# A planner that orders five engine queues: its durations, a price on idle TensorE, and other preferences among streams

## The chip, the cores and the metric

The kernel runs on one core of one Trainium2 chip. The metric is the time of one execution on the device in microseconds, lower is better. Each kernel's time is the median of several runs.

## The reference

One transformer layer on `x` of shape (2, 4096, 256) in float32, with one attention head of width 256, followed by a layer that processes only three quarters of the rows (cut):

```
qkv = x @ w_attn + b_attn; q, k, v = split(qkv, 3)
attn = softmax(q @ k.T / sqrt(256) + causal_mask)
x = layernorm(x + (attn @ v) @ w_proj + b_proj)
scores = x @ w_router
_, top_idx = top_k(scores, k=3072)            # of 4096 rows in each batch
out = x.at[top_idx].set(gelu(x[top_idx] @ w_block))
return layernorm(x + out)
```

## The kernel before

The work is cut into 16 groups: two batches of eight, each of 512 queries. Group g of a batch has 4(g+1) tiles of 128 keys by 512 queries, 288 tiles in all. Every float32 operand of the big products is split into a high and a low part, and three products (low by high, high by high, high by low) stand for one, so a tile of scores is six matmuls of up to 512 columns (L535, into one of two `sbank` banks), and a tile of values is six as well (L1134 to L1136, into `obank`; the first three groups of a batch use L1128 to L1130).

A group goes through these stages. *Project*: ScalarE and GpSimd split the rows of `x` (`xT`), TensorE makes queries and values (L535 into `fbank`). *Scores*: TensorE writes a bank, ScalarE copies it into one of 34 slots of `ring` (L955), VectorE masks it and keeps a running maximum (L992, L997). *Row maximum*: four transposes (L1030), a VectorE reduction, four transposes back (L1053). *Softmax*: VectorE subtracts (L1066), ScalarE takes the exponential (L1073) and rounds it to the high part (`parts`, L1080), VectorE makes the low part (`ring_lo`, L1085). *Values*: SyncE loads 256 KB per tile of keys into one of six slots (`vs`, L1103), TensorE multiplies. *Attention out*: ScalarE empties `obank` (L1194), residual, layer norm, router score. *ffn*: TensorE multiplies by `w_block` (L535 with `WB`), gelu on ScalarE, sum with `x1` on GpSimd (L1556), statistics on VectorE; `x1` and `y` go to scratch memory in DRAM. The 512-KB load of the residual rows of group G (L1177, stream "attention_out load") waits until GpSimd has made the sums of group G - 2 (`g_y`), because they share a buffer.

After the last group of a batch, a *search* finds the 3072nd largest router score in eight rounds: VectorE compares (L1668), TensorE counts with a matrix of ones (L1724), VectorE adds up and decides (L1679, L1685). Then rows are picked (L1917) and stored. The scratch rows of the second batch come back during the last group's values (`final_load`: two loads of 256 KB, L1850 and L1851, inside the stream "values load", one pair for every three tiles).

What the five engines do in which order isn't written by hand. Each step is put into a named *stream* of an engine (`at("act", "softmax exp", exp)`), and the order inside a stream is fixed. Before anything is emitted, `merged` lets every step run against a `Rehearsal` object that adds up a duration from `COSTS` (fixed part, time per element, delay until another engine sees the semaphore). `urgency` computes for each step the longest way to the end, and `planned` (L206) walks through time: for each engine it takes the step that can start earliest, and among equals the one with the longest way plus a preference for the stream:

```
picks.append((max(when + MARGIN_US.get(n, 0.0), free[e]),
              -urgent[e, n][place[e][n]] - PREFER_US.get(n, 0.0) - more, n, max(when, free[e])))
```

`when` is the time at which the semaphores allow the step, `free[e]` the time at which the engine is done with what it has; a margin makes a stream look later than it is; `more` and a delay come from `FAVOUR_US`, a few steps of the last groups (the gelu of group 13 is planned 8 us late and 20 us less urgent). So a preference decides only among steps that are all ready before the engine is. The result is one queue per engine, executed strictly in order on the chip with the same semaphores whatever the order is. The planner runs on the host when the program is built.

Of the kernel before, what the change touches and what calls it, by code (L numbers as in the profile page):

```python
# [53 lines left out]
DMA_US, DMA_BYTES_US, FIRST_BYTES_US = 2.0, 320e3, 250e3  # L54
START_US = .8
COLD_US, COLD, COLD_STREAMS = 4.0, 1.85, ()
TABLE_US = 1.28

PREFER_US = {"ffn flo": 100, "final load": 100, "project vhi": 100, "ffn store": 100, "last chain": 60,
             "last router": 60, "project qhi": 60, "attention_out residual": 60, "project qlo": 60,  # L60
             "attention_out stats": 60, "ffn fhi": 60, "attention_out score": 60, "row_max": 60,
             "final store": 60, "search first": 60, "scores copy": 30, "softmax hi": 30, "final pick": 30,
             "search": 30, "ffn stats": 15, "values load": 15, "prepare xlo": 8, "attention_out norm": 8,
             "row_max reduce": 4, "project xhi": 4, "project vlo": 4, "softmax lo": 4, "ffn gelu": 4,
             "project load": 4, "attention_out evac": 4, "prepare bias": 4, "scores hide": -4, "softmax exp": -4,
             "softmax z": -4, "final result": -4, "ffn add": -4, "ffn aggr": -8, "attention_out router": -8,
             "attention_out aggr": -8, "attention_out istd": -8, "last": -8, "final scale": -15, "final own": -15,
             "final choose": -30, "prepare": -30}
MARGIN_US = {"attention_out router": 3, "final scale": 3, "project xhi": 2, "ffn flo": 2, "final_roots": 2,
             "prepare bias": 1.5, "out": 1.5, "ffn store": 1.5, "scores hide": 1, "values load": 0.6,  # L70
             "ffn aggr": 0.6, "row_max reduce": 0.6, "values": 0.6, "project load": 0.3, "proj": 0.3,
             "attention_out stats": 0.3}

COSTS = {"pe": (.0, 1 / 2400, .2), "act": (.13, 1 / 1200, .14), "dve": (.09, 1 / 960, .12),
         "pool": (.35, 1 / 460, .1), "sp": (.45, 0.0, 0.0)}


class Rehearsal:
# [3 lines left out]
    def __init__(self, engine):  # L82
        self.engine = engine
        self.fixed, self.per_element, self.delay = COSTS[engine]
        self.waits, self.incs, self.time = {}, [], 0.0
# [37 lines left out]

    def activation(self, out, in_, func, bias=0.0, scale=1.0):
        self.table = {ACT.Gelu_apprx_tanh: "gelu", ACT.Exp: "exp"}.get(func)
        self.time += .15 * (not isinstance(scale, float)) + .1 * (not isinstance(bias, float))
        return self.work(out)

    def tensor_tensor(self, out, in0, in1, op):
# [5 lines left out]
        return self.work(out)  # L135

    def scalar_tensor_tensor(self, out, in0, scalar, in1, op0, op1, accum_out=None):
        return self.two(out, in0, in1)

    def copy_predicated(self, out, mask, data):  # L140
# [18 lines left out]
        return self.work(out)  # L159

    def tensor_tensor_reduce(self, out, in0, in1, scale, scalar, op0, op1, accum):
        self.time += .08
        return self.two(out, in0, in1)

    def tensor_tensor_scan(self, out, in0, in1, init, op0, op1):
# [40 lines left out]
def planned(todo, signalled, urgent, favours):  # L206


    reached = {name: [(0.0, 0)] for name in signalled}
    free = {e: START_US for e in todo}  # L210
    place = {e: {n: 0 for n in s} for e, s in todo.items()}
    orders = {e: [] for e in todo}
    times = {e: [] for e in todo}
    port, dma, table = START_US, START_US, "exp"

    def ready(waits):

        when = 0.0
        for name, value in waits.items():
            if name in signalled:  # L220
                r = reached[name]
                if r[-1][1] < value:
                    return None
                i = len(r) - 1
                while i and r[i - 1][1] >= value:
                    i -= 1
                when = max(when, r[i][0])
        return when

    for _ in range(sum(len(m) for s in todo.values() for m in s.values())):  # L230
        best = None
        for e in todo:
            picks = []
            for n, ops in todo[e].items():
                if place[e][n] < len(ops):
                    when = ready(ops[place[e][n]][1])
                    if when is not None:
                        more, later = favours.get((e, n, place[e][n]), (0.0, 0.0))
                        when += later
                        picks.append((max(when + MARGIN_US.get(n, 0.0), free[e]),  # L240
                                      -urgent[e, n][place[e][n]] - PREFER_US.get(n, 0.0) - more, n, max(when, free[e])))
            if picks:
                _, _, n, when = min(picks)
                if best is None or when < best[1]:
                    best = (e, when, n)
        if best is None:
            raise RuntimeError(f"no operation can start: {place}")
        e, when, n = best
        r = todo[e][n][place[e][n]][2]
        orders[e].append((n, place[e][n]))  # L250
        place[e][n] += 1
        if r.port:
            when = max(when, port)
        time = r.time * (COLD if n in COLD_STREAMS or e == "pe" and when < COLD_US else 1.0)
        if r.table and r.table != table:
            time, table = time + TABLE_US, r.table
        free[e] = when + time
        if r.port:
            port = when + time
        times[e].append((when, time, n))  # L260
        if r.bytes:
            dma = max(when + DMA_US, dma) + r.bytes / (DMA_BYTES_US if when > 10 else FIRST_BYTES_US)
        for t, name, by in r.incs:
            seen = max(reached[name][-1][0], dma if e == "sp" else when + (time - r.time) + t + r.delay)
            reached[name].append((seen, reached[name][-1][1] + by))
    return orders, times


def merged(streams, favours):

    todo = {e: {n: [] for n in s} for e, s in streams.items()}
    signalled = set()
    for e, named in streams.items():
        for n, makers in named.items():
            for make in makers:
                r = Rehearsal(e)
                make(r)
# [1776 lines left out]
```

## Time and profile before

| | |
|---|---|
| median of 3 runs | 961.22 us (958.93 to 964.9) |
| span of the profiled execution (first to last instruction) | 962.9 us |
| instructions | 15643 |
| TensorE busy | 934.3 us, 97% of the span |
| VectorE, ScalarE, GpSimd busy | 791.0, 637.6, 303.6 us (82%, 66%, 32%) |
| bytes moved by DMA | 155.84 MB, mean 162 GB/s |

The profiled execution's own time is given by its span alone; the runs' times are those of other executions. In the rows below PE is TensorE (matmuls), DVE VectorE, ACT ScalarE, POOL GpSimd and SP SyncE with its DMA queue.

### The profile page before, as it was taken

What the parts mean: (1) busy time and instruction counts of PE and PEld (TensorE: products, weight loads), DVE (VectorE), ACT (ScalarE), POOL (GpSimd) and SP (SyncE); (2) the same over time, 40 slices, a digit from 0 to 9 for tenths busy, and PEclk for the clock granted to TensorE, in tenths of its full rate; (3) what the DMA queues carried; (4) which work ended last, traced back from release to release, by engine and by line L of the source; (5) the groups of instructions that cost most, each with busy time, mean ns of one, the idle gap of its engine ahead of it and who ended that gap; (6) DMA issues with size and microseconds to landing.
All of it is one profiled execution on the core that took longest, in us unless ns stands there. A gap on an engine that the chain in (4) does not pass through costs nothing.

```text
span 962.9 us, 15643 instructions
## 1 busy us (share of the span) xinstructions
PE 934.3 (97%) x5018; PEld 799.2 (83%) x5018; DVE 791.0 (82%) x1494; ACT 637.6 (66%) x1009; POOL 303.6 (32%) x460
## 2 busy tenths in 40 slices
PE   9999999999999999999999999999999999998892
PEld 7889988888888888888889998888888888887671
DVE  5789886967976885699989898999899789489768
ACT  4467665764873776486757757586689577449794
POOL 3423231333220335414541253314212422131162
PEclk9999999999999999999999999999999999999996
DMA  6535344454364365488533633535769635347734
GB/s 212 166 114 171 113 141 122 120 158 126 101 184 116 102 187 155 132 255 277 175 109 94 199 108 110 164 102 172 247 223 295 212 106 153 99 144 241 264 128 175
DMA packets 89044, 155.84 MB, mean 162 GB/s; under 512 B 8442, under 2 KB 18300, under 8 KB 88964
## 3 DMA queue, kind: packets, MB, share of 16 engines
q1 hardware_dynamic: 88964, 154.85, 51.5%
q8 instruction: 41, 0.67, 0.3%
q14 instruction: 39, 0.32, 0.1%
HBM read 114.96 MB, written 39.86 MB: 161 GB/s over the span
## 4 chain that ended last, share of the span: by engine, by line
PE 93%; DVE 3%; DMA 1%; ACT 1%; issue 1%; DVEq 0%; POOL 0%; SPq 0%; ACTq 0%
PE sbank L535 38%; PE fbank L535 13%; PE obank L1134 11%; PE obank L1136 11%; PE obank L1135 10%; PE obank L1128 2%; PE obank L1130 2%; PE obank L1129 2%; DMA vs<-v_scratch 1%; PE fbank L1225 1%; PE mbank L1053 1%; PE mbank L1030 1%; DVE tail L1917 1%; PE fbank L1490 1%; DMA xraw<-xt 0%
## 5 line engine op out<-in xcount | busy, mean ns | idle before, releaser
L535 PE MATMUL sbank<-qT,xT 128*128 128x512 f32 (+2 forms) x1728 | 411.5, 378 | 0.2 <-issue 0.2
L535 PEld LDWEIGHTS sbank<-qT,xT 128*128 128x128 f32 x1728 | 304.9, 188 | 52.8 <-issue 0.6
L955 ACT COPY ring<-sbank 128x512 f32<-128x512 f32 (+3 forms) x286 | 156.2, 548 | 179.4 <-PE sbank L535 132.0
L1085 DVE TENSOR_TENSOR ring_lo<-ring,parts 128x1024 fp32r<-128x1024 f32 (+4 forms) x175 | 174.4, 1007 | 21.9 <-ACT parts L1080 21.3
L1134 PE MATMUL obank<-ring_lo,vs 128*128 128x512 f32 x476 | 182.5, 383 | 7.4 <-issue 3.5
L1136 PE MATMUL obank<-parts,vs 128*128 128x512 f32 x480 | 183.2, 382 | 0.0
L1135 PE MATMUL obank<-parts,vs 128*128 128x512 f32 x480 | 182.9, 381 | 0.0
L1080 ACT CAST parts<-ring 128x1024 fp32r<-128x1024 f32 (+4 forms) x175 | 144.8, 834 | 45.5 <-PE obank L1136 35.8
L1066 DVE TENSOR_TENSOR ring<-ring,mbank 128x1024 f32<-128x1024 f32 (+4 forms) x175 | 158.2, 944 | 7.3 <-PE mbank L1053 7.2
L1073 ACT ACTIVATE ring<-ring 128x1024 f32<-128x1024 f32 (+4 forms) x175 | 142.6, 842 | 21.6 <-DVE ring L1066 21.2
L997 DVE TENSOR_TENSOR runmax<-ring,runmax 128x1024 f32<-128x1024 f32 x84 | 106.6, 1269 | 59.3 <-ACT ring L955 58.6
L1134 PEld LDWEIGHTS obank<-ring_lo,vs 128*128 128x128 f32 x476 | 90.4, 190 | 25.1 <-issue 6.7
L1556 POOL TENSOR_TENSOR yb<-xres,yb 128x512 f32<-128x512 f32 x28 | 41.0, 1481 | 210.6 <-ACT yb L1542 80.1
L1136 PEld LDWEIGHTS obank<-parts,vs 128*128 128x128 f32 x480 | 90.9, 189 | 17.0
L1135 PEld LDWEIGHTS obank<-parts,vs 128*128 128x128 f32 x480 | 91.2, 190 | 16.1
L1186 POOL TENSOR_TENSOR xres<-xres,b_tot 128x512 f32<-128x512 f32 x32 | 49.0, 1554 | 67.5 <-DMA xres<-x 66.1
L839 POOL TENSOR_TENSOR xT<-xraw,xT 128x512 fp32r<-128x512 f32 x27 | 38.4, 1436 | 78.0 <-ACT xT L821 77.0
L1452 POOL TENSOR_TENSOR ot_sb<-ot_sb,yb 128x512 f32<-128x512 f32 x16 | 22.5, 1405 | 98.5 <-PE fbank L1225 80.6
L992 DVE TENSOR_TENSOR runmax<-ring,runmax 128x512 f32<-128x512 f32 (+3 forms) x74 | 44.9, 606 | 9.7 <-ACT ring L955 8.5
L535 PEld LDWEIGHTS fbank<-WV,xT 128*128 128x128 f32 x384 | 49.8, 191 | 2.3 <-issue 0.3
L535 PE MATMUL fbank<-WV,xT 128*128 128x256 f32 x384 | 51.2, 283 | 0.0
L535 PE MATMUL fbank<-xT,A 128*128 128x512 f32 x192 | 49.4, 393 | 0.2 <-POOL xT L839 0.2
(244 smaller groups left out, 1257.7 us busy)
## 6 DMA issues: line engine op xcount, KB each, us to landing
vs<-v_scratch SPq DMA_DIRECT2D x288, 256.0 KB, 2.9
v_scratch<-vnew SPq DMA_DIRECT2D x30, 512.0 KB, 3.1
xres<-x SPq DMA_DIRECT2D x16, 512.0 KB, 4.0
out<-tail SPq DMA_DIRECT2D x32, 256.0 KB, 2.8
x_scratch<-xres SPq DMA_DIRECT2D x14, 512.0 KB, 3.0
y_scratch<-yb SPq DMA_DIRECT2D x14, 512.0 KB, 4.1
tail<-x_scratch SPq DMA_DIRECT2D x28, 256.0 KB, 3.4
tail<-y_scratch SPq DMA_DIRECT2D x28, 256.0 KB, 4.0
```

Of the source, the lines that this page charges most:

```text
L535: mm = eng.matmul(o, lhs(lh, k), rhs(rh, k), start=n == 0, stop=n == len(todo) - 1)
L955: act.copy(slot(n)[:, c0:], sbank[n % NSS][:, c0:]).then_inc(a_copy, 1)
L992: dve.tensor_tensor(runmax[:, 0, c0:], slot(n)[:, c0:], runmax[:, 0, c0:], ALU.max).then_inc(v_max, 1)
L997: dve.tensor_tensor(runmax[:, :, :], slots(ns, 0), runmax[:, :, :], ALU.max).then_inc(v_max, 1)
L1066: dve.tensor_tensor(slots(ns, c0), slots(ns, c0), mbank[:, None, c0:].broadcast_to([P, len(ns), GQ - c0]), ALU.subtract).then_inc(v_z, 1)
L1073: act.activation(slots(ns, c0), slots(ns, c0), ACT.Exp, scale=SCALE).then_inc(a_exp, 1)
L1080: act.copy(hi_of(u), slots(ns, c0)).then_inc(a_hi, 1)
L1085: dve.tensor_tensor(slots_lo(ns, c0), slots(ns, c0), f32(hi_of(u)), ALU.subtract).then_inc(v_lo, 1)
L1134: pe.matmul(o, vh, lo_, start=i == 0, stop=False)
L1135: pe.matmul(o, vh, hi_, start=False, stop=False)
L1136: mm = pe.matmul(o, vl, hi_, start=False, stop=last)
L1186: pool.tensor_tensor(r[:, 2 * j:2 * j + 2], r[:, 2 * j:2 * j + 2], b_tot[:, None, :].broadcast_to([P, 2, C]), ALU.add).then_inc(g_xres, 1)
```

## The change

Nothing in the kernel's steps, tiles, buffers or semaphores is changed; `planned` gets other numbers and one more rule, so the five queues may come out in other orders. (1) The durations: fixed parts and times per element of every engine but SP, a few additions for forms of instruction. (2) The rule: when TensorE has waited over 1.3 us, its steps that start in the 3.5 us from then on are planned 1.85 times as long; before, that factor held for the first 4 us of the program alone. (3) New tables `PREFER_US` and `MARGIN_US`, 59 and 46 entries in the place of 45 and 16. Cut to the entries that matter below:

```diff
+IDLE_US, SLOW_US = 1.3, 3.5
-PREFER_US = {"ffn flo": 100, "final load": 100, "project vhi": 100, "ffn store": 100, "last chain": 60,
-             ... "scores copy": 30, "softmax hi": 30, ... "search": 30, "ffn stats": 15, ...
-             "softmax lo": 4, ... "softmax exp": -4, "softmax z": -4, ... "ffn add": -4, "ffn aggr": -8, ...}
+PREFER_US = {"row_max reduce": 286, ... "last chain": 142, "values load": 132, ... "scores copy": 99, ...
+             "softmax hi": 70, ... "ffn aggr": 48, ... "ffn gelu": -10, ... "softmax lo": -15, "softmax exp": -15,
+             ... "scores running": -45, ... "softmax z": -50, "search": -61, ... "ffn add": -150,
+             "project load": -165, "attention_out load": -212, ... "ffn stats": -300}
-MARGIN_US = {"attention_out router": 3, ... "out": 1.5, ... "proj": 0.3, ...}
+MARGIN_US = {"ffn aggr": 5, "ffn rows": 5, "ffn add": 5, ... "out": 1, "proj": 1, ... "softmax exp": 0.3, ...}
-COSTS = {"pe": (.0, 1 / 2400, .2), "act": (.13, 1 / 1200, .14), "dve": (.09, 1 / 960, .12),
-         "pool": (.35, 1 / 460, .1), "sp": (.45, 0.0, 0.0)}
+COSTS = {"pe": (.0, 1 / 2383, .2), "act": (.075, 1 / 1200, .17), "dve": (.065, 1 / 960, .13),
+         "pool": (.1, 1 / 445, .18), "sp": (.45, 0.0, 0.0)}
...
-        self.time += .15 * (not isinstance(scale, float)) + .1 * (not isinstance(bias, float))
+        self.time += .11 * (not isinstance(scale, float)) + .09 * (not isinstance(bias, float))
...
-    port, dma, table = START_US, START_US, "exp"
+    port, dma, table, slow = START_US, START_US, "exp", COLD_US
...
-        time = r.time * (COLD if n in COLD_STREAMS or e == "pe" and when < COLD_US else 1.0)
+        if e == "pe" and when > 2 * COLD_US and when - free[e] > IDLE_US:
+            slow = when + SLOW_US
+        time = r.time * (COLD if n in COLD_STREAMS or e == "pe" and when < slow else 1.0)
```

The other lines of the diff add .06 us to `scalar_tensor_tensor` and .01 us to `tensor_tensor_reduce`.

## Rows read from the trace of the kernel before

**Rows 1.** The page: busy time of TensorE, and its clock in 40 slices.
```profile
PE 934.3 (97%) x5018; PEld 799.2 (83%) x5018; DVE 791.0 (82%) x1494; ACT 637.6 (66%) x1009; POOL 303.6 (32%) x460
...
PEclk9999999999999999999999999999999999999996
```

**Rows 2.** The page: the chain that ended last, by engine.
```profile
PE 93%; DVE 3%; DMA 1%; ACT 1%; issue 1%; DVEq 0%; POOL 0%; SPq 0%; ACTq 0%
```

**Rows 3.** Busy time by stage (us, then each engine's busy us, granted clock, DMA).
```profile
50.00:425.00 375.00, 374.67 (x2014) 324.04 (x2013) 294.32 (x514) 242.56 (x377) 112.44 (x154) 1.00 0.47 143
425.00:850.00 425.00, 424.47 (x2303) 366.41 (x2302) 373.12 (x696) 290.79 (x457) 134.52 (x190) 1.00 0.54 167
...
869.00:877.00 8.00, 4.98 (x29) 4.11 (x27) 8.00 (x11) 7.91 (x11) 0.00 (x0) 1.00 0.55 177
877.00:881.00 4.00, 4.00 (x11) 3.17 (x12) 4.00 (x4) 3.97 (x6) 0.00 (x0) 0.57 0.87 296
881.00:894.00 13.00, 13.00 (x63) 10.84 (x62) 9.25 (x12) 10.79 (x13) 2.55 (x2) 1.00 0.90 293
894.00:901.00 7.00, 2.98 (x13) 1.89 (x12) 4.71 (x10) 5.93 (x10) 2.53 (x2) 1.00 0.75 268
901.00:905.00 4.00, 4.00 (x13) 3.12 (x12) 3.90 (x8) 0.03 (x1) 0.00 (x0) 0.57 0.35 119
905.00:924.00 19.00, 19.00 (x86) 15.70 (x85) 14.31 (x38) 17.32 (x28) 7.18 (x15) 1.00 0.91 308
```

**Rows 4.** Timeline of TensorE: start, us, what, [idle before, who ended it].
```profile
869.42 0.39 PE L1136 MATMUL obank<-parts,vs 128*128 128x512 f32 x1
871.42 0.47 PE L1134 MATMUL obank<-ring_lo,vs 128*128 128x512 f32 x1 [1.61 <-ACT ot_sb L1194]
...
876.97 0.47 PE L1134 MATMUL obank<-ring_lo,vs 128*128 128x512 f32 x1 [1.41 <-ACT parts L1080]
...
900.33 0.47 PE L1134 MATMUL obank<-ring_lo,vs 128*128 128x512 f32 x1 [3.52 <-issue]
...
935.00 1.90 PE L1524 MATMUL obank<-runmax,late_x 128*128 128x256 f32 x8
```

**Rows 5.** Timeline of ScalarE around the first of these gaps.
```profile
870.21 1.06 ACT L1194 COPY ot_sb<-obank 128x512 f32<-128x512 f32 x2
...
874.30 2.93 ACT L1080 CAST parts<-ring 128x1024 fp32r<-128x1024 f32 x3
```

**Rows 6.** Timeline of the DMA issues ahead of the gap at 896.8 us.
```profile
886.15 0.38 SPq L1177 DMA_DIRECT2D xres<-x  x1
...
894.74 7.93 SPq L1103 DMA_DIRECT2D vs<-v_scratch  x3
```

**Rows 7.** The chain that ended last, in order of time: start, us, what.
```profile
867.00 1.42 PE fbank L535 x12
...
887.02 8.03 DMA vs<-v_scratch
```

**Rows 8.** Timeline of GpSimd: the sums of group 13.
```profile
881.43 2.55 POOL L1556 TENSOR_TENSOR yb<-xres,yb 128x512 f32<-128x512 f32 x2 [22.62 <-issue]
```

**Rows 9.** Timeline of VectorE: two of the last search's eight rounds.
```profile
934.76 0.29 DVE L1679 TENSOR_REDUCE mbank<-fbank 128x15 f32<-128x120 f32 x1 [0.42 <-PE fbank L1724]
...
937.14 0.29 DVE L1679 TENSOR_REDUCE mbank<-fbank 128x15 f32<-128x120 f32 x1 [0.99 <-PE fbank L1724]
...
941.35 0.27 DVE L1679 TENSOR_REDUCE mbank<-fbank 128x15 f32<-128x120 f32 x1
...
943.09 0.29 DVE L1679 TENSOR_REDUCE mbank<-fbank 128x15 f32<-128x120 f32 x1
```

**Rows 10.** Timeline of VectorE near the start: one form, twice.
```profile
17.07 0.28 DVE L963 TENSOR_TENSOR ring<-ring,mask 128x128 f32<-128x128 f32 x1
...
18.14 1.20 DVE L963 TENSOR_TENSOR ring<-ring,mask 128x128 f32<-128x128 f32 x1
```

**Rows 11.** Timeline of GpSimd beside them.
```profile
17.91 2.57 POOL L839 TENSOR_TENSOR xT<-ring,xT 128x512 fp32r<-128x512 f32 x2 [10.02 <-ACT xT L821]
```

More of the change, by code:

```diff
@@ L56 @@
 COLD_US, COLD, COLD_STREAMS = 4.0, 1.85, ()
+IDLE_US, SLOW_US = 1.3, 3.5
 TABLE_US = 1.28
-PREFER_US = {"ffn flo": 100, "final load": 100, "project vhi": 100, "ffn store": 100, "last chain": 60,
[L60 to L72, printed above, removed]
-COSTS = {"pe": (.0, 1 / 2400, .2), "act": (.13, 1 / 1200, .14), "dve": (.09, 1 / 960, .12),
-         "pool": (.35, 1 / 460, .1), "sp": (.45, 0.0, 0.0)}
+PREFER_US = {"row_max reduce": 286, "prepare keys": 206, "project qhi": 190, "prepare bias": 181,
+             "search first": 160, "ffn scale": 157, "final choose": 150, "ffn rows": 146, "last chain": 142,
+             "values load": 132, "final scale": 126, "attention_out istd": 113, "scores copy": 99, "final sums": 97,
+             "final store": 94, "final result": 93, "attention_out norm": 90, "project vhi": 84, "project qlo": 79,
+             "attention_out score": 71, "softmax hi": 70, "final load": 69, "project xlo": 54,
+             "attention_out ot": 51, "ffn aggr": 48, "attention_out stats": 40, "ffn sums": 40, "row_max": 32,
+             "late load": 31, "prepare late": 28, "prepare xlo": 11, "ffn fhi": 10, "ffn store": 7,
+             "project vlo": -7, "late": -8, "ffn gelu": -10, "prepare": -11, "softmax lo": -15, "softmax exp": -15,
+             "attention_out router": -15, "ffn flo": -17, "attention_out evac": -20, "final_roots own": -30,
+             "scores running": -45, "attention_out aggr": -48, "softmax z": -50, "search": -61, "last router": -71,
+             "project vstore": -72, "last": -87, "final_roots": -93, "attention_out store": -98, "project xhi": -100,
+             "attention_out residual": -111, "scores hide": -130, "final own": -132, "final pick": -136,
+             "ffn add": -150, "project load": -165, "attention_out load": -212, "bias columns": -229,
+             "ffn stats": -300}
@@ new lines @@
+MARGIN_US = {"ffn aggr": 5, "ffn rows": 5, "ffn add": 5, "attention_out residual": 5, "attention_out istd": 5,
+             "late": 5, "attention_out router": 3, "final choose": 3, "late load": 3, "attention_out aggr": 3,
+             "project xhi": 2, "project xlo": 2, "attention_out store": 2, "ffn flo": 1.5, "prepare bias": 1.5,
+             "bias columns": 1.5, "final store": 1.5, "final_roots own": 1.5, "final pick": 1.5, "final scale": 1,
+             "out": 1, "proj": 1, "prepare keys": 1, "last router": 1, "final_roots": 0.6, "ffn store": 0.6,
+             "project load": 0.6, "attention_out stats": 0.6, "ffn scale": 0.6, "ffn sums": 0.6, "final own": 0.6,
+             "prepare late": 0.6, "attention_out ot": 0.6, "prepare xlo": 0.6, "scores running": 0.6,
+             "project vstore": 0.6, "attention_out score": 0.6, "scores hide": 0.3, "values": 0.3,
+             "project qhi": 0.3, "prepare": 0.3, "softmax z": 0.3, "project vlo": 0.3, "softmax exp": 0.3,
+             "last": 0.3, "ffn fhi": 0.3}
@@ L137, in scalar_tensor_tensor @@
     def scalar_tensor_tensor(self, out, in0, scalar, in1, op0, op1, accum_out=None):
+        self.time += .06
         return self.two(out, in0, in1)
@@ L161, in tensor_tensor_reduce @@
     def tensor_tensor_reduce(self, out, in0, in1, scale, scalar, op0, op1, accum):
-        self.time += .08
+        self.time += .09
         return self.two(out, in0, in1)
```

## The prediction

> **What bounds the kernel now.** I read the page's busy times first, then the chain, then busy time by stage, and last the timelines of the stages that aren't full. TensorE is busy for 97% of the span at a full clock in nearly every slice [rows 1], and the chain that ends last runs through it for 93% [rows 2]: whatever another engine does costs time only where TensorE has to wait for it. By stage there is hardly such a place in the first 850 us: of 375 us in one long stretch and 425 us in the next TensorE is idle for 0.33 and 0.53 us [rows 3]. The idle time is near the end. Between 869 and 877 us it is 8.00 - 4.98 = 3.02 us, between 894 and 901 us 7.00 - 2.98 = 4.02 us [rows 3]. Behind each of the first two the granted clock is 0.57 for 4 us, a mix of the levels 2.4 and 1.2 GHz, in which TensorE loses 0.43 x 4.00 = 1.72 us though it shows as busy [rows 3]. So the first gap costs 4.74 us and the second 5.74 us. Busy time cannot show whether the matmuls themselves could run closer together, but the change neither removes nor reshapes any, so I count only waits.
>
> The gap at 869 us, call it A, has two waits of TensorE: 1.61 us for ScalarE to empty `obank` of group 14 before group 15 may write it, then 1.41 us for the high part of the softmax, L1080 [rows 4]. ScalarE is busy for 7.91 of the 8 us [rows 3]: the two copies take 1.06 us, then come exponentials and, from 874.30, three casts in a row, 2.93 us [rows 5]. The last scores are done by then, so TensorE has no other work to put in.
>
> The gap at 894 us, call it B, has one long wait of 3.52 us that the trace can put down to no engine [rows 4]; the chain has a DMA there, a `vs` load issued at 887.02 that needs 8.03 us [rows 7], and three later `vs` issues stretch over 7.93 us [rows 6]. Just ahead of it SyncE issued the 512-KB load of group 15's residual [rows 6], which the sums of group 13 at 881.43 to 883.98 [rows 8] release. The DMA engines are busy at 0.90 in that stage and at 0.91 in the next [rows 3].
>
> From 924 us on the end is a serial chain: group 15's attention out, the search in eight rounds, picks and stores. TensorE's waits there are a result of VectorE's chain.
>
> **The change, part by part.** No instruction is added or removed and no wait; only the places in five queues move. The cost is therefore what the new orders do to the waits above, and I can't read the new orders off the diff. I bound each wait from both sides: it may vanish or stay; that new waits come is the slower rival below, since no row of the trace before can bound them.
>
> *The durations.* They are nearer to the trace for GpSimd: an addition of 128x512 was planned at .35 + 512/460 = 1.46 us, now at .1 + 512/445 = 1.25 us; two of them in a row take 2.55 us, 1.28 each [rows 8]. A cast of 128x1024 on ScalarE was .13 + 1024/1200 = 0.98 us and is now 0.93; three take 2.93, 0.98 each with the last one's full end [rows 5]. A TensorE step of 512 columns grows by 0.6%. None of these is a cost on the chip; better durations make the planner's waits more like the real ones. I take zero for this part by itself.
>
> *The price on idle TensorE.* The planner didn't know the 1.72 us behind A and B. It still chooses step by step and doesn't look ahead, so the price by itself moves little; what it does is let preferences be judged by a time that contains it. Zero by itself as well.
>
> *The preferences and margins.* These move steps. For A, the block product of group 13 in `fbank`, 12 matmuls in 1.42 us, runs at 867.00, right before the last values of group 14 [rows 7]. Run 2.4 us later, it fills 1.42 of the 1.61 us, and its reader, the gelu of group 13, is planned late anyway. With one gap left I expect the clock to hold. I take 1.61 + 1.72 = 3.33 us of A's 4.74; the wait for the casts stays, because ScalarE has no free time there and "scores copy" (99) and "softmax hi" (70) now stand even further above "softmax exp" (-15). Bounds: 0 and 4.74.
>
> For B, the 512-KB load must lie after the sums of group 13 and before the residual is needed, inside the last group's values. There a tile of values takes six matmuls; 86 in 19.00 us [rows 3] make 1.33 us a tile with 256 KB, 198 GB/s, and a pair of `final_load`s per three tiles, 512 KB in 4.0 us, adds 131 GB/s: 329 GB/s wanted. Moved are 293 GB/s at a share of 0.90 and 308 at 0.91 [rows 3], which is 326 to 338 GB/s at a full share. So there is next to no room for another 512 KB, and another order shifts the load, but can't make it free. Six slots of `vs` buffer some 8 us; whether that covers it depends on where in the rhythm the load falls. I take half, 2.87 us of 5.74. Bounds: 0 and 5.74. (The Trainium skill, DMA: Bandwidth & Descriptors, section Specifications, gives a fabric ceiling of 435 GB/s. By that the wanted 329 GB/s would leave a quarter free, B would be an accident that any order can mend, and the sum below would be 2.87 us better. The share of 0.9 at some 300 GB/s in this trace speaks against it; I go by the trace.)
>
> For the middle, 0.33 + 0.53 = 0.86 us, I take 0.4. In the search, two rounds are 937.14 - 934.76 = 2.38 us apart, others 943.09 - 941.35 = 1.74 us [rows 9]: a late block product of 1.90 us on TensorE [rows 4] stood ahead of the count, and VectorE was idle for 0.99 us. Eight rounds at up to 0.64 us over the shortest bound this by 0 and some 2 us; "last chain" goes from 60 to 142 and "ffn stats" from 15 to -300, which favours the chain, "search" from 30 to -61, which doesn't. I take 1.0.
>
> The sum is 3.33 + 2.87 + 0.4 + 1.0 = 7.6 us, against the profiled execution: 962.9 - 7.6 = 955.3 us. The median of the runs is 1.7 us below that span, so 961.2 - 7.6 = 953.6 us.
>
> **The rivals.** *All of it.* A, B, the middle and 1.5 us of the search go: 4.74 + 5.74 + 0.86 + 1.5 = 12.8 us, 948.4 us. It is near the least that orders can reach, since TensorE's work stays. Against it: the casts in A and the DMA share in B.
>
> *The orders do not change where it matters.* A preference decides only among steps that are all ready. In A the queue of ScalarE is full of steps that depend on one another, and in B the rhythm of the loads is fixed inside one stream and the late gelu is fixed by a table that is not changed. Then only the middle and the search move: 0 to 3 us, 958 to 962, say 960.
>
> *Slower: holes like A at other group changes.* "softmax z" falls from -4 to -50, "softmax exp" from -4 to -15 and "softmax lo" from 4 to -15, while "scores copy" rises from 30 to 99. ScalarE then serves the coming group's scores before the present group's softmax; VectorE does the statistics last. The scores of group G + 1 run out sooner, TensorE reaches the change of groups with values that aren't ready, and each such place costs what A costs, 3.02 us and 1.72 us for the clock. The present plan has none of it in the earlier changes from 50 us on, as the 0.86 us show. Two such places (9.5 us) eat the gain; four make 953.6 + 19.0 = 972.6 us. For it: VectorE is busy for 373.12 of 425 us in the second half [rows 3], so a late step isn't caught up quickly. Against it: the planner sees these waits, with better durations than before.
>
> *VectorE becomes the bound through GpSimd.* The same addition on VectorE takes 0.28 us and, while a large GpSimd step runs beside it, 1.20 us [rows 10, 11]: 0.92 us per collision. In the stretch from 425 to 850 us VectorE has 51.9 us free [rows 3], 56 collisions more than now. GpSimd's 134.52 busy us there [rows 3] at 1.28 hold at most 105 such steps, and the planner keeps a time for this port. It decides from about half of them, and then only slowly; I give it a place inside the slower case, not one of its own. (The Trainium skill, SBUF — State Buffer, section SBUF: two separate sides, says that the pair of ports is locked for the whole instruction and the other engine waits; by that a GpSimd step moved onto a VectorE step always costs the latter its whole remaining length, the worse end of my price.)
>
> **How the numbers follow.** Forecast, most of A and half of B gone, 949 to 957.5 us: 0.45. All of it, 945.5 to 949: 0.15. No change where it matters, 957.5 to 962.5: 0.24. Slower, from 962.5 up, mostly 966 to 985: 0.16. The range from 946 to 969 leaves out a little of the second case and two thirds of the last. Faster by over 1%, below 951.6 us, is nearly all of the second case and a third of the first: 0.15 + 0.15 = 0.30. Slower by over 1%, over 970.8, is 0.11 of the last case; with what I can't see of five new queues I say 0.15. The rest, 0.55, is within 1%, about what a measurement of this kernel can tell from no change (its three runs lie 0.6% apart).
>
> **What would show it.** For A: in the new trace TensorE's wait for L1194 at the change from group 14 to 15 is under 0.5 us, with a block product standing between the groups, and no slice of half clock there; wrong if a wait of over 1.3 us remains. For B: the longest wait of TensorE during the last values is under 2 us; wrong if a `vs` load again takes 8 us. For the search: no two rounds over 2.1 us apart. For the slower case: TensorE's idle time between 50 and 850 us, now 0.86 us, grows to several us, at changes of groups, with slices of half clock behind. The prediction is wrong as a whole if the end of the values moves by less than 3 or more than 12 us, or if the chain behind them, 962.9 - 924 = 38.9 us now, grows.

## The result, and the profile after

The changed kernel is slower: 983.81 us median (981.35 to 985.4, 4 runs) against 962.55 us for the kernel before on the same chip, ratio 1.0229, 95% interval 1.0199 to 1.0259. Line numbers after L75 are 14 higher than before. The page first (busy times, clock slices, the chain that ended last); it answers to [rows 1, 2].

```profile
PE 940.9 (96%) x5018; PEld 799.9 (81%) x5018; DVE 791.3 (81%) x1494; ACT 629.4 (64%) x1007; POOL 300.9 (31%) x460
...
PEclk9999999999999999999999999999999999998996
...
PE 71%; DVE 12%; issue 5%; ACT 4%; DMA 4%; POOL 3%; SPq 0%; DVEq 0%; ACTq 0%; POOLq 0%
```

VectorE has the same work, 791 us, but the chain now runs through it for 12%, not 3%: TensorE waits for the others. Where, the stages tell; the columns are those of [rows 3].

```profile
50.00:850.00 800.00, 787.70 (x4237) 676.87 (x4236) 659.47 (x1184) 521.96 (x824) 239.95 (x340) 1.00 0.48 152
...
50.00:75.00 25.00, 23.21 (x133) 20.37 (x132) 22.23 (x54) 17.23 (x32) 12.94 (x15) 1.00 0.37 120
...
525.00:575.00 50.00, 45.83 (x297) 40.97 (x296) 45.80 (x110) 31.85 (x54) 12.43 (x21) 1.00 0.40 130
...
700.00:775.00 75.00, 70.02 (x349) 58.16 (x347) 65.15 (x115) 56.48 (x95) 16.29 (x26) 1.00 0.75 247
...
885.00:894.00 9.00, 5.56 (x30) 4.46 (x28) 9.00 (x10) 8.26 (x14) 0.00 (x0) 1.00 0.63 197
894.00:901.00 7.00, 5.59 (x15) 4.41 (x15) 7.00 (x8) 7.00 (x9) 0.00 (x0) 0.51 0.57 200
...
906.00:940.00 34.00, 31.57 (x144) 25.54 (x143) 21.92 (x52) 30.22 (x54) 13.79 (x24) 1.00 0.87 292
```

From 50 to 850 us TensorE is idle for 800 - 787.70 = 12.30 us; before it was 0.33 + 0.53 = 0.86 us [rows 3]. Three stretches hold 1.79 + 4.17 + 4.98 = 10.94 us of it. The last matmul of the values starts at 940.2 us instead of 923.6 (timelines of TensorE, before and after):

```profile
923.57 0.39 PE L1136 MATMUL obank<-parts,vs 128*128 128x512 f32 x1
...
940.18 0.40 PE L1150 MATMUL obank<-parts,vs 128*128 128x512 f32 x1
```

That is 16.6 us later. 11.4 of it are this new idle time, and idle time ahead of 50 us and behind 850 us changes by 0.2 in all. The other 4.9 us count as busy, 919.0 us up to the values' end instead of 914.1, though the matmuls are the same; waits too short to show as idle would look like this, but no view here shows them. The chain behind the values is 982.7 - 940.2 = 42.5 us long, 3.2 more than before (39.3). Whom TensorE waits for (us in total, times, longest us):

```profile
PE mbank L1044 <- DVE runmax L1006: 6.5, 4, 3.0
PE obank L1148 <- issue: 3.9, 3, 1.5
...
PE obank L1148 <- ACT ot_sb L1208: 1.9, 1, 1.9
PE sbank L549 <- ACT ring L969: 1.8, 2, 1.2
PE obank L1148 <- ACT parts L1094: 1.4, 1, 1.4
```

The first line is new: the transposes of the row maximum wait for VectorE's running maximum; in the same list of the kernel before there is no such line. The first of them can be followed through four queues (start, us, what, idle time before and who ended it):

```profile
62.81 1.22 DVE L994 TENSOR_TENSOR runmax<-ring 128x1024 f32<-128x1024 f32 x1
...
66.76 0.18 DVE L1379 SCALAR_TENSOR_TENSOR score<-hw,rs_h 128x4 f32<-128x4 f32 x1 [0.89 <-POOL rs_h L1174]
...
67.19 2.48 DVE L1011 TENSOR_TENSOR runmax<-ring,runmax 128x1024 f32<-128x1024 f32 x2
69.71 0.69 DVE L1015 TENSOR_TENSOR runmax<-runmax 128x512 f32<-128x512 f32 x1
70.44 1.42 DVE L1006 TENSOR_TENSOR runmax<-ring,runmax 128x512 f32<-128x512 f32 x2
...
62.20 1.89 POOL L1169 TENSOR_SCALAR roots<-mv_h 128x4 f32<-128x4 f32 x1 [2.99 <-DVE mv_h L1270]
64.17 1.35 POOL L1170 TENSOR_TENSOR roots<-roots,half 128x4 f32<-128x4 f32 x1
65.60 0.20 POOL L1171 TENSOR_TENSOR roots<-roots 128x4 f32<-128x4 f32 x1
...
66.45 0.20 POOL L1174 TENSOR_TENSOR rs_h<-roots 128x4 f32<-128x4 f32 x1
...
67.30 1.18 POOL L1779 TENSOR_TENSOR froots<-mv_h,rs_h 128x4 f32<-128x4 f32 x1
...
67.25 1.10 ACT L1357 ACTIVATE xres<-xres,rstd,rs_h 128x256 f32<-128x256 f32 x2 [2.01 <-POOL rstd L1311]
68.25 0.56 ACT L969 COPY ring<-sbank 128x512 f32<-128x512 f32 x1
...
69.71 0.57 ACT L969 COPY ring<-sbank 128x512 f32<-128x512 f32 x1
...
71.91 0.66 PE L1044 MATMUL mbank<-ident,runmax 128*128 128x128 f32 x4 [1.79 <-DVE runmax L1006]
```

GpSimd makes the reciprocal roots of group 0 in a chain of eight steps of 4 elements. A free one takes 0.20 us; the one at 62.20, begun under VectorE's steps with two operands in SBUF, takes 1.89, and at 67.30 again 1.18 beside the running maximum. The chain ends at 67.22, 5.02 us after its start. The planner gives it, by the diff, 8 x .109 + .8 for the power + 7 x .18 = 2.93 us; by the old durations it was 4.37. VectorE's score step (L1379), which stands ahead of the last maxima in VectorE's queue, has VectorE idle for 0.89 us until the chain's sixth step (`rs_h`, L1174) is done; from 66.76 VectorE goes from step to step without idle time, and the end of its last maximum, 71.86, releases TensorE's transposes. That is the path that sets the time here. ScalarE's normalization waits 2.01 us for the same chain and the copies of the scores stand behind it in ScalarE's queue, but the last of them is done at 69.71 + 0.57 = 70.28, while VectorE is busy until 70.40. VectorE's own steps are late too: its two maxima at 67.19 take (69.71 - 67.19) / 2 = 1.26 us each and are planned at .065 + 1024/960 = 1.13 us. Each reads what the one before wrote; steps of that size that don't depend on one another follow each other every 1.14 us (before, three `ring_lo` subtractions at 875.65 take 3.49 us, one alone 1.21).

### The profile page after: what moved, and what is told of

Its sections match the earlier page's. It is cut to its first block, busy times and chain, and to the rows that moved or that the text cites. A ratio compares the mean times of both kernels' runs of the same rounds, so it can differ in the third digit from the quotient of the medians.

```text
span 982.7 us, 15644 instructions
## 1 busy us (share of the span) xinstructions
PE 940.9 (96%) x5018; PEld 799.9 (81%) x5018; DVE 791.3 (81%) x1494; ACT 629.4 (64%) x1007; POOL 300.9 (31%) x460
## 4 chain that ended last, share of the span: by engine, by line
PE 71%; DVE 12%; issue 5%; ACT 4%; DMA 4%; POOL 3%; SPq 0%; DVEq 0%; ACTq 0%; POOLq 0%
PE sbank L549 28%; PE fbank L549 9%; PE obank L1148 9%; PE obank L1150 9%; PE obank L1149 9%; DVE ring L1080 2%; DMA out<-tail 1%; DMA tail<-y_scratch 1%; ACT ring L1087 1%; DVE ring_lo L1099 1%; DVE runmax L1011 1%; ACT parts L1094 1%; PE obank L1142 1%; PE obank L1144 1%; PE obank L1143 1%
## 5 line engine op out<-in xcount | busy, mean ns | idle before, releaser
L1099 DVE TENSOR_TENSOR ring_lo<-ring,parts 128x1024 fp32r<-128x1024 f32 (+4 forms) x175 | 179.5, 1037 | 33.8 <-ACT parts L1094 33.5
L1080 DVE TENSOR_TENSOR ring<-ring,mbank 128x1024 f32<-128x1024 f32 (+4 forms) x175 | 155.9, 943 | 3.1 <-PE mbank L1067 3.0
L1570 POOL TENSOR_TENSOR yb<-xres,yb 128x512 f32<-128x512 f32 x28 | 37.6, 1365 | 146.2 <-ACT yb L1491 105.0
```

Source lines behind the costliest of these rows:

```text
L1080: dve.tensor_tensor(slots(ns, c0), slots(ns, c0), mbank[:, None, c0:].broadcast_to([P, len(ns), GQ - c0]), ALU.subtract).then_inc(v_z, 1)
L1099: dve.tensor_tensor(slots_lo(ns, c0), slots(ns, c0), f32(hi_of(u)), ALU.subtract).then_inc(v_lo, 1)
```

## The experiments

Each run's ratio is against the kernel before, measured beside it (its median between 959.6 and 961.6 us). "Idle" is TensorE's idle time from 50 to 850 us and "root" ScalarE's whole wait for the reciprocal roots, both from that run's trace. The kernel before itself has medians from 959.6 to 962.55 us, so the ratios are what to compare.

| run | median us | ratio, 95% interval | idle us | root us |
|---|---|---|---|---|
| (before) | 962.55 | 1 | 0.87 | 7.9 |
| (after) | 983.81 | 1.0229, 1.0199 to 1.0259 | 12.30 | 23.6 |
| new_costs_old_tables | 981.1 | 1.0205, 1.0154 to 1.0256 | 6.59 | 24.3 |
| new_costs_but_pool | 977.31 | 1.0161, 1.0123 to 1.0199 | 6.32 | 4.1 |
| before_dve_new | 976.17 | 1.0175, 1.0141 to 1.0209 | 6.71 | 9.1 |
| before_act_new | 967.46 | 1.0087, 1.0058 to 1.0117 | 2.02 | 8.4 |
| before_act_125 | 968.21 | 1.0093, 1.0069 to 1.0117 | 1.73 | 10.4 |
| before_pool_36 | 964.72 | 1.0033, 1.0011 to 1.0055 | 2.11 | 5.8 |
| before_dve_long | 966.68 | 1.0051, 1.003 to 1.0073 | 2.49 | 7.8 |
| after_no_newton | 980.69 | 1.0197, 1.0154 to 1.0239 | 7.62 | 8.8 |
| after_quarter_adds | 978.39 | 1.0187, 1.0169 to 1.0205 | 10.15 | 21.4 |
| after_cut_both | 976.45 | 1.0138, 1.0103 to 1.0174 | 7.06 | 0.8 |
| after_small_stores | 981.33 | 1.0207, 1.0179 to 1.0236 | 10.35 | 24.6 |
| after_all_cuts | 969.39 | 1.008, 1.0049 to 1.0111 | 4.14 | 0.8 |
| before_no_newton | 961.85 | 1.0003, 0.9983 to 1.0023 | 0.71 | 0.3 |
| before_quarter_adds | 958.7 | 0.9986, 0.9969 to 1.0003 | 0.33 | 5.9 |
| before_all_cuts | 958.38 | 0.9975, 0.996 to 0.999 | 0.33 | |
| fitted_3 | 965.36 | 1.0043, 1.0028 to 1.0059 | 4.01 | 1.9 |
| fitted_1 | 959.69 | 0.9972, 0.9956 to 0.9988 | 2.41 | 3.0 |
| fitted_12 | 958.76 | 0.9984, 0.9972 to 0.9996 | 1.70 | 3.9 |

**One part alone.** The change's durations and its price on idle TensorE under the old tables (shown against the changed kernel, cut), then the same with GpSimd's old durations (shown against the run before it):

```diff
-PREFER_US = {"row_max reduce": 286, "prepare keys": 206, "project qhi": 190, "prepare bias": 181,
...
+PREFER_US = {"ffn flo": 100, "final load": 100, "project vhi": 100, "ffn store": 100, "last chain": 60,
...
+MARGIN_US = {"attention_out router": 3, "final scale": 3, "project xhi": 2, "ffn flo": 2, "final_roots": 2,
...
```

> The change's durations and its price on idle TensorE, with the preferences and margins of before. Theory 1 (the planned durations of GpSimd's chains of small steps are now too short, since nothing in them stands for VectorE holding the shared port, so ScalarE queues behind a reciprocal root that isn't there yet): this half alone carries the loss, 970 to 985 us, with TensorE waiting for transposes of the row maximum at changes of groups. Theory 2 (the new preferences serve the coming group's scores ahead of the present group's softmax): the loss goes with the tables, so 958 to 965 us here.

```diff
-         "pool": (.1, 1 / 445, .18), "sp": (.45, 0.0, 0.0)}
+         "pool": (.35, 1 / 460, .1), "sp": (.45, 0.0, 0.0)}
```

> As the run before it, with GpSimd's old durations (.35 fixed) put back and nothing else. Theory 1: the loss of the run before goes, 956 to 964 us. Theory 2: within 0.5% of the run before. A third reading, that any new set of durations under tables that were chosen for another one loses some per cent by chance: both runs slow, 968 to 985 us, in no fixed order.

Without the new tables the loss is as large, 2.05%; theory 2, the preferences as its cause, falls. But it doesn't lie in the same places: TensorE's idle time from 50 to 850 us is 6.59 us, not 12.30, its waits for the running maximum are 2.7 us, not 6.5, and the chain behind the values is 45.8 us long, not 42.5. Putting GpSimd's old durations back does exactly one thing that theory 1 said: ScalarE's wait for the roots goes from the first of these rows to the second (the first is of new_costs_old_tables).

```profile
ACT xres L1347 <- POOL rstd L1301: 24.3, 12, 3.6
```
```profile
ACT xres L1347 <- POOL rstd L1301: 4.1, 4, 1.3
```

But the time falls by 3.8 us alone, and the two intervals overlap. So the wait for the roots is real, what it costs is at most small, and theory 1 as the whole cause falls too; the third reading, a loss by chance, has both runs in its range. Two runs are missing: the new tables with the old durations, and the price on idle TensorE by itself.

**Which engine's durations, and how much is chance.** In the kernel before, one engine's numbers at a time (cut to the line of constants):

```diff
-COSTS = {"pe": (.0, 1 / 2400, .2), "act": (.13, 1 / 1200, .14), "dve": (.09, 1 / 960, .12),
+COSTS = {"pe": (.0, 1 / 2400, .2), "act": (.13, 1 / 1200, .14), "dve": (.065, 1 / 960, .13),
```

> The kernel before with only VectorE's durations of the change (fixed .065 for .09, delay .13 for .12, .06 and .01 more for two of its operations). Theory 3 (the new durations are those of steps that run alone; what VectorE loses to GpSimd on the shared port, which the old, longer durations partly covered, is now in no duration, so VectorE falls behind its plan and the row maximum comes late): most of the loss is here, 970 to 985 us, with waits for the row maximum at changes of groups. Theory 4 (the plan before is one good draw, and any change of its numbers gives another draw, that is mostly worse): 963 to 985 us, about as much as the two runs with tiny changes lose.

```diff
+COSTS = {"pe": (.0, 1 / 2400, .2), "act": (.075, 1 / 1200, .17), "dve": (.09, 1 / 960, .12),
```

> The kernel before with only ScalarE's durations of the change (fixed .075 for .13, delay .17 for .14, .11 and .09 for a scale and a bias that are columns). Theory 3: ScalarE has no port to share, so little is lost, 959 to 966 us. Theory 4: 963 to 985 us.

```diff
+         "pool": (.36, 1 / 460, .1), "sp": (.45, 0.0, 0.0)}
```

> The kernel before with .36 for .35 in GpSimd's fixed duration, a change of no meaning. Theory 3: 959 to 964 us, as before. Theory 4: at least one of this run and the next is 967 us or more.

```diff
+COSTS = {"pe": (.0, 1 / 2400, .2), "act": (.125, 1 / 1200, .14), "dve": (.09, 1 / 960, .12),
```

> The kernel before with .125 for .13 in ScalarE's fixed duration, a change of no meaning. Theory 3: 959 to 964 us, as before. Theory 4: at least one of this run and the one before is 967 us or more.

A change of .005 us in one constant costs 0.9%, as much as the whole new set for ScalarE (0.9%), and one of .01 us 0.3%; theory 4 forecast this and theory 3 didn't. So the place of a plan among its neighbours is worth several microseconds by itself, and the kernel before stands well in it. VectorE's durations cost 1.75%, without the price on idle TensorE and in the range of both theories; that is outside the scatter as far as two tiny changes show it. In that run's trace too TensorE waits for the running maximum:

```profile
PE obank L1135 <- issue: 5.1, 1, 5.1
PE mbank L1031 <- DVE runmax L993: 3.8, 4, 1.6
```

The opposite, VectorE's durations made longer (with the change's rate for TensorE):

```diff
-COSTS = {"pe": (.0, 1 / 2400, .2), "act": (.13, 1 / 1200, .14), "dve": (.09, 1 / 960, .12),
+COSTS = {"pe": (.0, 1 / 2383, .2), "act": (.13, 1 / 1200, .14), "dve": (.11, 1 / 960, .12),
```

> The kernel before with VectorE's durations made longer (.11 for .09 fixed) and TensorE's made right (1/2383), tables unchanged. Theory 5: longer planned durations leave room, so in spite of the new draw 958 to 965 us, where the shorter ones of the change gave 976. Theory 4: no better than the tiny changes, 964 to 980 us.

966.68 us lies just above theory 5's range and inside theory 4's: no better than a tiny change, but 9.5 us better than the shorter durations.

**The orders held, the suspect cut out.** In the next eight the planner sees the unchanged steps, so all queues keep their orders, and only the step that is sent to the chip is shortened (in one place it is made to wait). First the Newton steps of the roots, in both kernels:

```diff
+            if not isinstance(pool, Rehearsal):
+                pool.tensor_tensor(rs, v, half[:, 0:rs.shape[-1]], ALU.pow).then_inc(done, 1)
+                return
             link(pool.tensor_tensor(root, v, half[:, 0:rs.shape[-1]], ALU.pow))
```

> The changed kernel with every queue's order held, and the Newton step (three or four small GpSimd steps) left out of the chains for the reciprocal roots (groups before the last two for the second of the two chains), so that the roots are less exact and each chain takes about what the planner thought. Theory 1: the waits for the roots shrink and with them what follows, 968 to 977 us, at least 7 us below the changed kernel, and the first jump of 2 us near 70 us is gone. Theory 2: these steps are beside the path, 981 to 984 us.

> The same steps left out of the kernel before, its orders held. Theory 1: there the plan gave the chains as long as they take, so little waits for them: 959 to 962 us, under 3 us gained. Theory 2: 960 to 962 us too; a gain as large as that of the changed kernel would say that GpSimd's chains are a cost of both orders and no cause of the difference.

3 us come back, not 7, and the intervals with and without the cut overlap; before nothing comes back. The wait for the roots falls from 23.6 to 8.8 us, yet TensorE's wait for the running maximum stays (6.8 us in 4). Near 70 us it is 2.00 us, where it was 1.79: VectorE no longer waits for `rs_h` and starts its last two maxima 0.93 us earlier, but GpSimd's low part of group 7 is earlier as well, 70.19 for 71.37, and beside it they take 2.49 us for 1.42. Then the large additions:

```diff
+                n = C if isinstance(pool, Rehearsal) else C // 4
+                y, x1 = y_pair(G, j)[:, :, 0:n], x1_pair(G, j)[:, :, 0:n]
+                pool.tensor_tensor(y, x1, y, ALU.add).then_inc(g_y, 1)
```

> The changed kernel with every queue's order held; of GpSimd's large additions (of the residual and the bias, of the rows ahead of the ffn, and of the ffn's result) only a quarter of the columns is added, the rest is left out, so that GpSimd holds the port that it shares with VectorE for some 0.4 us where it held it for 1.3 to 1.5. Theory 3 (the new plan has every step at the duration that it has alone, and the collisions at the port make VectorE and GpSimd late against it): much of the loss goes, 966 to 976 us, and TensorE's waits for the row maximum, 6.5 us, fall below 3 us. Rival (the new queues wait for one another whatever the durations): 980 to 984 us.

> The same columns left out of the kernel before, its orders held. Theory 3: its waits in the middle are small already, 958 to 961 us, at most 3 us gained. Rival: the same as the changed kernel gains, so that the difference between the two orders stays over 18 us.

5 us come back (0.4% by the ratios, whose intervals just overlap) against 1 in the control, and 6.2 us of waits for the running maximum stay: theory 3 has the direction and a third of the size that it wanted. With the chains cut to two or three steps as well (GpSimd's busy time from 50 to 850 us falls from 239.95 to 91.44 us):

```diff
+            if not isinstance(pool, Rehearsal):
+                pool.tensor_scalar(rs, var, 1.0, EPS, ALU.mult, ALU.add).then_inc(done, 1)
+                return
```

> The changed kernel with every queue's order held, with the additions on a quarter of the columns as before and, beyond that, GpSimd's chains for the roots cut down to two or three small steps each (the roots themselves are left out), so that the chains are far shorter than the planner thought and GpSimd hardly holds the port. Theory 3 in its widest form (GpSimd, its port and its chains together are the loss): 964 to 971 us. Theory 5 (the new plan puts every engine's steps at their shortest durations, ScalarE's, VectorE's, GpSimd's and the loads' alike, so that many paths end at the same moment and taking one away lets the next one set the time): 972 to 979 us, less than the sum of the two single cuts more than that of the quarter alone.

7.4 us of 21 are back, as theory 5 said. What is left near 70 us shows a second form of the same thing, in the timeline of that run:

```profile
68.67 0.69 DVE L1015 TENSOR_TENSOR runmax<-runmax 128x512 f32<-128x512 f32 x1
69.39 3.32 DVE L1006 TENSOR_TENSOR runmax<-ring,runmax 128x512 f32<-128x512 f32 x2
...
69.03 3.13 POOL L853 TENSOR_TENSOR xT<-xraw,xT 128x512 fp32r<-128x512 f32 x2 [4.07 <-ACT xT L835]
```

Two maxima of 128x512 need 1.66 us each, where one alone needs 0.69, since GpSimd's low part of group 7 has come ahead of them to the port. In the changed kernel this low part starts at 71.37, behind the same maxima; with GpSimd's chains cut it is there at 69.03, and VectorE loses 3.32 - 1.42 = 1.90 us. The planner reckons with the port for steps of that size, but no semaphore holds the planned order there, so an engine that is early can cost the other as much as one that is late. The last cuts test this place and the one near 710 us:

```diff
+                n = C if b or isinstance(sp, Rehearsal) else C // 4
+                sp.dma_start(out[b, u].rearrange("p (t c) -> p t c", t=2)[:, :, 0:n], y[:, :, 0:n]).then_inc(st_o[u % 2], 16)
```

> The changed kernel with every queue's order held; of the outputs of batch 0 only a quarter of the columns is stored, the rest is left out, so that the buffers come free earlier and SyncE, which waits 3.0 to 3.4 us for such a store ahead of each pair of final loads, reaches the loads sooner. Theory 5 with its second place (ScalarE and VectorE are sent into the final steps of batch 0 before their loads are there, and the row maximum queues behind them): TensorE's wait of 3.0 us near 710 us goes or falls below 1 us, 976 to 980 us. Rival: that place is late for another reason, 982 to 985 us with the wait still there.

```diff
+                    if G == 7 and not isinstance(pool, Rehearsal):
+                        pool.wait_ge(v_max, max_done[2])
```

> The changed kernel with every queue's order held and all cuts together: a quarter of GpSimd's additions, the short chains in place of the roots, a quarter of the stores of batch 0, and one wait more, by which GpSimd's low part of group 7 comes after the last running maximum of group 2, as it was planned, and so doesn't hold the port against it near 70 us. Theory 5: the waits near 70 and near 710 us both go, 964 to 971 us, some 5 to 9 us below the run without the last two cuts (976.45). Rival: 973 to 977 us.

> The kernel before with the same cuts, its orders held (without the wait for group 7, since its low part already comes at another time). Theory 5: hardly anything waits for what is cut, 955 to 960 us. Rival (the cuts are a cost of both orders alike): below 950 us.

The stores alone miss: near 710 us TensorE still waits 2.5 us, and what makes the maximum late there stays open. All cuts together reach 969.39 us, as expected, with 2.9 us in two waits for the running maximum instead of 6.5 in four; near 70 us the wait is 0.9 us instead of 2.8. 14.4 us of the changed kernel's time hang on what was cut, 2.6 us of the kernel before. (The one wait undoes a collision that the cut chains had brought about, and the kernel before, with little to wait for in the middle, has little to win there.)

**Tables chosen by measured durations.** The last three use the unchanged program with other numbers in the tables. Each candidate's orders were played back off the chip with durations that the traces show for each kind of step and with the port's collisions, and the best were built; only their times on the chip are used here. Of 25 entries that fitted_1 moves in the tables of before, the largest are "last router" from 60 to -30, "last chain" from 60 to -15, "project vhi" from 100 to 30 and "attention_out load" from 0 to 60, and margins of 2 and 3 us for "final load" and "final sums"; two of GpSimd's constants change:

```diff
-         "pool": (.35, 1 / 460, .1), "sp": (.45, 0.0, 0.0)}
+         "pool": (.346, 1 / 460, .132), "sp": (.45, 0.0, 0.0)}
```

> The program before with longer planned durations for VectorE (.11 fixed), TensorE's rate of the change, and preferences and margins chosen anew by the end of each plan's orders played back with the step durations and port collisions of the traces taken so far, instead of the planner's own durations. Theory 5: what makes a plan good is that its order survives the real durations, so this one is 950 to 959 us, below both kernels. Theory 4 (any change of the numbers is a new draw, mostly worse): 963 us or more.

> A second set of preferences and margins chosen in the same way, with the durations of before nearly unchanged (GpSimd's fixed .346, its delay .132). Theory 5: 952 to 960 us, a little less good than the run before it. Theory 4: 963 us or more.

> A third set of preferences and margins, searched on from those of fitted_1 with the same durations; the orders were played back with loads that take 0.6 us longer as well, because final loads landed later than planned near 710 us. Theory 5: 953 to 959 us, below fitted_1's 959.7. Theory 4: within a per cent of the kernel before on either side, 956 to 968 us, with no order among the fitted ones.

fitted_3 misses; fitted_1 and fitted_12 are below both kernels, by 0.3% and 0.2% with 1 outside both intervals. By its ratio fitted_12 isn't below fitted_1, as was expected, and its time lies in the range of theory 4 as well. With three draws this supports theory 5 and doesn't prove it. In fitted_1 the timeline of TensorE marks only these two waits between 860 and 920 us (under them a stage):

```profile
873.56 0.47 PE L1121 MATMUL obank<-ring_lo,vs 128*128 128x512 f32 x1 [1.61 <-ACT ot_sb L1181]
879.03 0.47 PE L1121 MATMUL obank<-ring_lo,vs 128*128 128x512 f32 x1 [1.41 <-ACT parts L1067]
...
880.00:920.00 40.00, 39.87 (x188) 32.87 (x187) 35.97 (x70) 37.76 (x58) 14.91 (x26) 1.00 0.94 318
```

Gap A is there as before, 1.61 and 1.41 us; gap B is gone, while DMA moves 318 GB/s.

## Why the prediction was wrong

**The step that failed is "The durations": "I take zero for this part by itself."** With the price on idle TensorE, which I took at zero too, it costs 2.05% or 20 us (new_costs_old_tables), as much as the whole change; VectorE's durations alone, without the price, cost 1.75%. The reason given was that better durations make the planner's waits more like the real ones. I judged them by [rows 5, 8], by steps that run back to back. For the addition they are nearer (1.25 us planned for 1.28); the cast's row, 2.93 / 3 = 0.98 us, is the old figure and not the new 0.93. (A TensorE step of 512 columns grows by 0.7%, not 0.6%.)

What the runs show in its place: the plan is executed with chains, where each step reads what the one before wrote (1.26 us for 1.13 planned), and with collisions at the port (1.18 to 1.89 us for 0.20; 1.66 for 0.69). The old fixed parts were .025 us longer for each step of VectorE and .25 for each of GpSimd. That this room is what the kernel before lives on is argued, and it covers only a part: the old numbers give 1.16 us for the 1.26 and 4.37 us for the 5.02. Shown are:

- The durations and the price lose as much as the change.
- Of the sets that were run alone VectorE's loses most (1.75%).
- GpSimd's durations carry the wait for the roots (24.3 against 4.1 us).
- 14.4 - 2.6 = 11.8 of the 21 us in the held order hang on GpSimd's port and chains, the stores and the one wait.

These cuts shorten steps and not their planned durations, so they show what is waited for and not that it was planned too short. Not settled are the other 9.5, and how much of the whole is merely a worse draw, since a constant moved by .005 us costs 0.9%. That many paths end at the same moment (theory 5) fits the small return of each single cut, but no run isolates it.

"I count only waits" left out a term as well: 4.9 of the 16.6 us by which the values end later are in no wait that the views show.

**The slower rival** had the right sign and place: "holes like A at other group changes", TensorE's idle time between 50 and 850 us up from 0.86 to 12.30 us. I gave it 0.16. Its mechanism is not what the trace shows: it put the holes down to values that aren't ready because new preferences push the softmax behind the copies, while the largest waits are for the running maximum, and the old tables lose as much. That the new tables make the middle worse, 12.30 us for 6.59, and the end better isn't ruled out. As to its price, I charged 1.72 us of clock to each hole; the granted clock is 1.00, the upper of its two levels (2.4 GHz), in the three stretches that hold the new waits, the longest of them 3.0 us. But in after_no_newton, with the same orders, waits of 2.00 and 2.94 us at the first and the last of these places are followed by a lower clock (stages of that run):

```profile
72.00:76.00 4.00, 3.95 (x19) 3.47 (x20) 3.15 (x6) 1.05 (x1) 1.14 (x1) 0.69 0.24 80
76.00:80.00 4.00, 4.00 (x27) 3.78 (x26) 2.34 (x7) 2.12 (x6) 0.00 (x0) 0.89 0.36 135
...
708.00:712.00 4.00, 4.00 (x16) 3.52 (x17) 3.93 (x13) 1.39 (x3) 1.76 (x2) 0.57 0.57 172
```

The last row is 0.43 x 4.00 = 1.72 us, the price that I had charged. So a hole may or may not cost it, and no run shows what decides. The argument against it, "the planner sees these waits, with better durations than before", was the failed step once more.

**VectorE and the port.** I placed this inside the slower case, and priced VectorE's step beside a large GpSimd step alone [rows 10, 11]. The port works the other way too, on steps of four elements, which the planner's rule leaves out (`size >= 256` in `work`); that price was missing. The page cited there (the Trainium skill, SBUF — State Buffer, section SBUF: two separate sides) says that whichever engine starts first holds the pair for its whole instruction; the 1.18 us beside a maximum of 1.24 us agree with it.

**A: wrong.** I took 3.33 of 4.74 us off. TensorE waits 1.9 us for L1208 and twice more, 1.5 and 1.4 us, and the clock is at 0.51, nearly the lower level (1.2 GHz), for 7 us, of which TensorE is busy for 5.59: 0.49 x 5.59 = 2.74 us. With 3.44 + 1.41 = 4.85 us idle that makes 7.59 us where A cost 4.74. Both waits, for the evictions and for the casts, stand in the fitted orders too (1.61 and 1.41 us in fitted_1, 1.3 and 1.4 in fitted_12): none of these orders fills A. In fitted_1 the clock is 1.00 from 870 to 880 us and in the stage behind it, so there A costs its 3.02 us alone.

**B: right, and could have been right in full.** The longest wait in the last values is 1.3 us, no `vs` load takes over 5.5 us, and from 906 to 940 us TensorE is idle for 34.00 - 31.57 = 2.43 us at a full clock: 3.3 of the 5.74 us are gone, where I took 2.87. My bound, "next to no room for another 512 KB", was too tight: fitted_1 moves 318 GB/s at a share of 0.94 with TensorE busy for 39.87 of 40 us. B also goes in before_quarter_adds, with the orders of before (its longest such wait is 0.3 us): it hung on timing, not on the rhythm alone. (That is what the sentence on the fabric ceiling of the Trainium skill, DMA: Bandwidth & Descriptors, section Specifications, had made of it, an accident; the ceiling itself isn't reached here: the most that a stage shown here moved is 318 GB/s.) Whether B was in every execution before can't be seen, as one is profiled.

**The search: wrong.** Two counts are still 957.07 - 954.45 = 2.62 us apart, where I expected at most 2.1; a late block product of 1.89 us at 954.68 stands ahead of the second count, as it did before:

```profile
954.45 0.29 DVE L1693 TENSOR_REDUCE mbank<-fbank 128x15 f32<-128x120 f32 x1 [0.37 <-PE fbank L1738]
957.07 0.28 DVE L1693 TENSOR_REDUCE mbank<-fbank 128x15 f32<-128x120 f32 x1
```

**As a whole**, both conditions that I named for a wrong prediction hold: the values' end moved by 16.6 us, to the wrong side, and the chain behind it grew by 3.2 us.

## What to carry to other kernels

A planner's durations that come nearer to single steps need not make a better plan: here the plans with VectorE's durations of undisturbed steps lost 1.6 to 2.3%. Longer ones are no cure by themselves (before_dve_long lost 0.5%); taking them from the steps in place, with their chains and collisions, is what two of three fitted plans speak for. Before a gain or a loss is put down to a table, change a constant by a hundredth of a microsecond or less and run it: here that alone moved the time by 0.3 to 0.9%. And where two engines share a port, queues don't hold the order there; if the order matters, a wait must.

## What the hardware showed that I had not expected

A GpSimd step of 128x4 takes 0.20 us and, beside VectorE's steps with both operands in SBUF, 1.18 to 1.89 us, about as long as what runs beside it. The same wait of TensorE can cost clock in one run and none in another: 2.95 us near 710 us left the granted clock at 1.00 in the changed kernel, 2.94 us at the same place were followed by 0.57 for 4 us in after_no_newton. At A, 1.61 and 1.41 us were followed by 0.57 before and by 1.00 in fitted_1.
